# Queries of later tiles made in thirds and copied under masks, in a six-stage transformer kernel

## The reference

```python
q = (x @ Wq + bq).reshape(1, B * N, H, hd)            # H, hd = 16, 16
kv = (cond @ Wkv + bkv).reshape(1, -1, 2, H, hd)
...
q = _fq_sym(q, axis=-1)       # round(q/s), s = max|q|/127 over a head
k = _fq_sym(k, axis=-1)
v = _fq_sym(v, axis=2)
attn = jnp.einsum('bhqd,bhkd->bhqk', q, k)
attn = jax.nn.softmax(attn.astype(jnp.float32), axis=-1)
attn = _fq_unsigned(attn, axis=-1)
out = jnp.einsum('bhqk,bhkd->bhqd', attn, v)
return out @ Wp + bp
```

## Time and profile before

| | us |
|---|---|
| median of 3 runs | 464.66 |
| lowest and highest | 461.84, 470.23 |
| the profiled execution | 469.39 |
| its span, first to last instruction | 467.6 |
| TensorE busy in the span | 379.8 (81%) |
| VectorE busy | 302.8 (65%) |
| ScalarE busy | 213.5 (46%) |
| GpSimd busy | 133.1 (28%) |

### The profile page before, as it was taken

One profiled execution on the slowest core, in us unless ns is written; L12 is line 12 of the kernel. 1 busy time (PEld: TensorE's weight loads), 2 busy tenths in 40 slices (PEclk: granted clock), 3 DMA queues, 4 the chain that ended last, 5 costly groups with the idle time before them and its releaser, 6 DMA issues.

```text
span 467.6 us, 6836 instructions
## 1 busy us (share of the span) xinstructions
PE 379.8 (81%) x2363; PEld 225.6 (48%) x2387; DVE 302.8 (65%) x624; ACT 213.5 (46%) x546; POOL 133.1 (28%) x236
## 2 busy tenths in 40 slices
PE   5997878479977999989947558677666998999993
PEld 2646466334434566556624234324344644555562
DVE  4994398958734687878866989979861452122235
ACT  2655131272245765856435669898971311111100
POOL 8248756828671000020053441211110000000002
PEclk9979795779999799999976898988985698999997
DMA  8992101490000000000024656997996004012211
GB/s 249 329 359 22 1 2 1 147 393 1 0 1 0 1 2 1 1 2 1 2 53 63 131 104 114 175 167 145 153 164 203 0 0 147 22 45 64 50 45 45
DMA packets 75521, 39.84 MB, mean 85 GB/s; under 512 B 64160, under 2 KB 71264, under 8 KB 75040
## 3 DMA queue, kind: packets, MB, share of 16 engines
q1 hardware_dynamic: 73184, 39.35, 34.4%
q0 software_dynamic: 2304, 0.07, 1.5%
HBM read 21.58 MB, written 2.88 MB: 52 GB/s over the span
## 4 chain that ended last, share of the span: by engine, by line
PE 55%; DVE 19%; issue 9%; DMA 6%; ACT 5%; POOL 5%; SPq 0%; POOLq 0%; DVEq 0%; ACTq 0%
PE ps L819 28%; PE ps L1266 6%; PE ps L1002 5%; PE ps L1017 4%; DVE area_a L1642 4%; PE ps L1140 3%; DMA area_b<-area_b 3%; POOL deltas L506 2%; ACT area_b L744 2%; DVE area_b L1543 2%; PE ps L996 2%; PE ps L1036 2%; PE ps L1165 2%; DVE stats L1390 2%; DMA area_b<-deltas 1%
## 5 line engine op out<-in xcount | busy, mean ns | idle before, releaser
L744 ACT ACTIVATE area_b<-area_a,small 128x1024 int16<-128x1024 f32 x64 | 72.9, 1141 | 23.9 <-POOL small L578 20.1
L1642 DVE CUSTOM_DVE_ANT_0 area_a<-ps,zero,small 128x1024 f32<-128x1024 f32 x64 | 79.5, 1276 | 6.7 <-ACT area_b L744 4.5
L714 ACT ACTIVATE area_a<-ps,small 128x256 f32<-128x256 f32 (+1 forms) x128 | 51.9, 435 | 29.4 <-DVE small L1534 27.2
L475 POOL TENSOR_SCALAR var_eps<-meanvar 128x1 f32<-128x1 f32 x24 | 6.7, 280 | 199.8 <-DVE meanvar L1391 199.7
L819 PE MATMUL ps<-xT_odd,early 128*128 128x512 f32 x128 | 59.4, 612 | 0.0
L1714 DVE TENSOR_TENSOR area_b<-ps,area_b 128x512 f32<-128x512 f32 x16 | 11.1, 691 | 55.5 <-ACT area_b L794 55.5
L1140 PE MATMUL ps<-area_b 128*128 128x512 bf16 x86 | 29.0, 417 | 15.5 <-DVE small L1642 14.1
L1534 DVE TENSOR_REDUCE small<-ps 128x4 f32<-128x1024 f32 (+1 forms) x24 | 29.3, 1221 | 18.5 <-PE ps L1002 18.2
L794 ACT ACTIVATE area_b<-ps 128x512 f32<-128x512 f32 x16 | 9.5, 596 | 67.1 <-PE ps L819 67.1
L819 PE MATMUL ps<-area_b,xT_even 128*128 128x512 f32 x64 | 31.2, 632 | 9.0 <-ACT area_b L691 9.0
L819 PEld LDWEIGHTS ps<-xT_odd,early 128*128 128x128 f32 x128 | 24.9, 197 | 27.0 <-issue 26.5
(11 more groups left out here) (274 smaller groups left out, 685.3 us busy)
## 6 DMA issues: line engine op xcount, KB each, us to landing
early<-in_w_up_dram SPq DMA_DIRECT2D x1, 4096.0 KB, 16.0
area_b<-gates_out SPq DMA_DIRECT2D x16, 256.0 KB, 3.1
deltas<-area_b SPq DMA_DIRECT2D x1, 2112.0 KB, 17.6
area_b<-deltas SPq DMA_DIRECT2D x2, 1024.0 KB, 5.8
area_a<-in_w_down_dram SPq DMA_DIRECT2D x1, 2048.0 KB, 9.0
early<-in_ctxT_dram SPq DMA_DIRECT2D x1, 1024.0 KB, 13.7
early<-in_ctx_dram SPq DMA_DIRECT2D x1, 1024.0 KB, 13.9
early<-in_w_qkv_dram SPq DMA_DIRECT2D x2, 384.0 KB, 5.4
```

Source lines behind the costliest of these rows:

```text
L714: a = act.activation(p1[:, n % 2, x * nk * P:(x + 1) * nk * P], scores1(n)[:, x * nk * P:(x + 1) * nk * P], ACT.Exp, bias=nmx1[:, n % 2, x ...
L744: act.activation(px[:, u % PX, :], sx[u % 3], ACT.Exp, bias=nbx[:, u:u + 1], accum_out=zx[:, i, h:h + 1]).then_inc(sem("px_ready"), 1)
L1642: dve.tensor_tensor_reduce(sx[u % 3], bank(2 * (u % 2), 2), zero[:].broadcast_to([P, B * M]), qsc[:, i, h:h + 1], LOWEST, ALU.add, ALU.max ...
```

## The change

- Queries of tiles 1 to 3 are made eight units apart in place of five. `quantise_queries` is cut into `take_queries`, `scale_queries`, `round_queries` at steps 5, 6, 7; `stack_queries` into three at steps 8, 9, 10; turning and copying come at step 11, as does `add_bias`.
- All of their PSUM is in bank 4; `turn` of the units for ScalarE keeps bank 5 alone. `turn_x4` no longer waits for `res4_ready`; a wait for it stands before `apply` of the second tile.
- `take_even` and `take_odd` read all 128 partitions and multiply by a column of `half_sel` (1 in one half of the partitions, 0 in the other), so they write the zeros themselves. `take_odd` now waits for `take_even`. The memsets of `qTx` and `qT_first` go; `qstack` has two places, cleared once in stage 4.
- The last local tile: `turn_z1` comes behind `scores(0)`, `spread_z1` behind `scores(2)`, `take_z1` between maxima 0 and 1, `add1` one unit later, `norm_scale` three later.

The diff, cut to its core:

```diff
+        half_sel = sb("half_sel", [P, 2])
...
-        qstack = carve("a", 0, [TT, HX * KW], BF16)
+        qstack = carve("a", 0, [2, HX * KW], BF16)
...
         def later_tile(u, step):
-            i, at = divmod(u - step, 5)
+            i, at = divmod(u - step, 8)
         def by_scalar(u):
...
+            pool.memset(half_sel[:], 1.0)
...
+            link(select(half_sel[:, 0:1], [[0, 1]], KW - 1, -1, ALU.is_ge, 0.0))
+            link(select(half_sel[:, 1:2], [[0, 1]], -KW, 1, ALU.is_ge, 0.0))
...
-            def stack_queries(i):
-                pool.wait_ge(sem("q_rounded"), i + 1)
-                stack = qstack[:, i, :].rearrange("p (h w) -> p h w", w=KW)
+            def stack_queries(i, k):
+                if k == 0:
+                    pool.wait_ge(sem("q_rounded"), i + 1)
+                if k == 0 and i >= 2:
+                    pool.wait_ge(sem("qT_ps"), i - 1)
+                stack = qstack[:, i % 2, :].rearrange("p (h w) -> p h w", w=KW)
-                for k in range(3):
-                    q = pool.tensor_scalar(stack[:, :, k * DHX:(k + 1) * DHX], heads, -127.0, None, ALU.max)
-                q.then_inc(sem("qstack_ready"), 1)
+                pool.tensor_scalar(stack[:, :, k * DHX:(k + 1) * DHX], heads, -127.0, None, ALU.max).then_inc(sem("qstack_ready"), 1)
...
-                            stack_queries(0)
+                            for k in range(3):
+                                stack_queries(0, k)
-                    pool.wait_ge(sem("o1_ps"), len(items1) // 2)
-                    pool.memset(qstack.rearrange("p i (h w) -> p (i h) w", w=KW)[:, HX:, 3 * DHX:KW], 0.0)
                     for u in range(TT * HX):
-                        if u < 4:
-                            pool.memset(qTx[:, 2 * u:2 * u + 2], 0.0).then_inc(sem("qTx_cleared"), 1)
-                        if u == 4:
+                        if u == 6:
-                        if later_tile(u, 6):
-                            add_bias(later_tile(u, 6))
-                        if later_tile(u, 7):
-                            stack_queries(later_tile(u, 7))
+                        for k in range(3):
+                            if later_tile(u, 8 + k):
+                                stack_queries(later_tile(u, 8 + k), k)
+                        if later_tile(u, 11):
+                            add_bias(later_tile(u, 11))
...
-                    pool.memset(qT_first[:], 0.0).then_inc(sem("first_cleared"), 1)
-                    pool.memset(qstack[:, 0, :], 0.0)
+                    pool.memset(qstack, 0.0)
...
-                        act.wait_ge(sem("first_cleared"), 1)
             def take_x4(i):
-                act.activation(xT[0][:, :, i * P:(i + 1) * P], bank(7)[:, 0:D].rearrange("p (c t) -> p c t", c=DC),
+                act.activation(xT[0][:, :, i * P:(i + 1) * P], bank(7 if i == 0 else 4)[:, 0:D].rearrange("p (c t) -> p c t", c=DC),
             def take_even(i, b):
-                dst = qT_first[0:KW, :, 0, :] if i == 0 else qTx[0:KW, :, 0, i * P:(i + 1) * P]
-                act.activation(dst, bank(b)[0:KW].bitcast(BF16).rearrange("p (c t) -> p c t", c=HX // 2),
-                               ACT.Copy).then_inc(sem("qT_even"), 1)
+                dst = qT_first[:, :, 0, :] if i == 0 else qTx[:, :, 0, i * P:(i + 1) * P]
+                act.activation(dst, bank(b).bitcast(BF16).rearrange("p (c t) -> p c t", c=HX // 2),
+                               ACT.Copy, scale=half_sel[:, 0:1]).then_inc(sem("qT_even"), 1)
             def stage5():
                 for u in range(TT * HX):
...
-                    if later_tile(u, 8):
-                        act.wait_ge(sem("qTx_cleared"), 4)
-                        take_even(later_tile(u, 8), 7)
+                    if later_tile(u, 11):
+                        take_even(later_tile(u, 11), 4)
...
-                act.activation(pTx[u % PT], bank(4 + n % 2).bitcast(I16), ACT.Copy).then_inc(sem("pTx_act"), 1)
+                act.activation(pTx[u % PT], bank(5).bitcast(I16), ACT.Copy).then_inc(sem("pTx_act"), 1)
             def evac_sums(i):
...
             def turn_x4(i):
-                if i:
-                    pe.wait_ge(sem("res4_ready"), TT)
-                    mm = pe.transpose(bank(7)[:, c * P:(c + 1) * P], x_tok[0][:, i, c * P:(c + 1) * P], ident[:])
+                    mm = pe.transpose(bank(7 if i == 0 else 4)[:, c * P:(c + 1) * P], x_tok[0][:, i, c * P:(c + 1) * P], ident[:])
             def project_q(i):
-                dense(bank(7)[:, D:2 * D], tile_of(4, i), lambda d: wqx[:, d, :]).then_inc(sem("qx_ps"), 1)
+                dense(bank(7 if i == 0 else 4)[:, D:2 * D], tile_of(4, i), lambda d: wqx[:, d, :]).then_inc(sem("qx_ps"), 1)
             def turn_q(i, b):
-                pe.wait_ge(sem("qstack_ready"), i + 1)
+                pe.wait_ge(sem("qstack_ready"), 3 * (i + 1))
-                    mm = pe.transpose(bank(b).bitcast(BF16)[:, c * P:(c + 1) * P], qstack[:, i, c * P:(c + 1) * P], ident_b[:])
+                    mm = pe.transpose(bank(b).bitcast(BF16)[:, c * P:(c + 1) * P], qstack[:, i % 2, c * P:(c + 1) * P], ident_b[:])
             def stage5(turn_z1, spread_z1, project1):
...
-                    if n > 2:
-                        pe.wait_ge(sem("pTx_act"), n - 2)
+                    if n > 1:
+                        pe.wait_ge(sem("pTx_act"), n - 1)
-                        mm = pe.transpose(bank(4 + n % 2).bitcast(BF16)[:, k * P:(k + 1) * P],
+                        mm = pe.transpose(bank(5).bitcast(BF16)[:, k * P:(k + 1) * P],
...
-                for u in range(3):
-                    scores(u)
+                scores(0)
+                turn_z1(TT - 1)
+                scores(1)
+                scores(2)
+                spread_z1(TT - 1)
                 for u in range(units + 3):
-                    if u == 0:
-                        turn_z1(TT - 1)
-                    if u == 1:
-                        spread_z1(TT - 1)
-                    if later_tile(u, 8):
-                        turn_q(later_tile(u, 8), 7)
+                    if later_tile(u, 11):
+                        turn_q(later_tile(u, 11), 4)
...
-                        pe.wait_ge(sem("qT_even"), TT)
-                        pe.wait_ge(sem("qT_odd"), TT)
+                        pe.wait_ge(sem("res4_ready"), TT)
...
-                        dve.wait_ge(sem("first_cleared"), 1)
...
-            def quantise_queries(i):
-                scale = DHX ** -0.5
-                flat = qx[:, i, :]
-                heads = flat.rearrange("p (h d) -> p h d", d=DHX)
+            def take_queries(i):
-                TTN(out=flat, in0=bank(7)[:, D:2 * D], in1=bqx[:], op=ALU.add).then_inc(sem("qx_ready"), 1)
+                TTN(out=qx[:, i, :], in0=bank(7 if i == 0 else 4)[:, D:2 * D], in1=bqx[:], op=ALU.add).then_inc(sem("qx_ready"), 1)
-                link(dve.tensor_reduce(qam[:, i, :], heads, AX.X, ALU.max, apply_absolute_value=True))
-                link(TS(qsc[:, i, :], qam[:, i, :], scale / 127, 1e-8, ALU.mult, ALU.max))
+                link(dve.tensor_reduce(qam[:, i, :], qx[:, i, :].rearrange("p (h d) -> p h d", d=DHX), AX.X, ALU.max,
+                                       apply_absolute_value=True))
+            def scale_queries(i):
+                heads = qx[:, i, :].rearrange("p (h d) -> p h d", d=DHX)
+                link(TS(qsc[:, i, :], qam[:, i, :], DHX ** -0.5 / 127, 1e-8, ALU.mult, ALU.max))
-                link(TS(flat, flat, scale, ROUND, ALU.mult, ALU.add))
+            def round_queries(i):
+                flat = qx[:, i, :]
+                link(TS(flat, flat, DHX ** -0.5, ROUND, ALU.mult, ALU.add))
+            def quantise_queries(i):
+                take_queries(i)
+                scale_queries(i)
+                round_queries(i)
             def take_odd(i, b):
-                dve.wait_ge(sem("qT_ps"), i + 1)
-                dst = qT_first[KW:2 * KW, :, 1, :] if i == 0 else qTx[KW:2 * KW, :, 1, i * P:(i + 1) * P]
-                dve.tensor_copy(dst, bank(b)[KW:2 * KW].bitcast(BF16).rearrange("p (c t) -> p c t", c=HX // 2)).then_inc(sem("qT_odd"), 1)
+                dve.wait_ge(sem("qT_even"), i + 1)
+                dst = qT_first[:, :, 1, :] if i == 0 else qTx[:, :, 1, i * P:(i + 1) * P]
+                TS(dst, bank(b).bitcast(BF16).rearrange("p (c t) -> p c t", c=HX // 2), half_sel[:, 1:2], None,
+                   ALU.mult).then_inc(sem("qT_odd"), 1)
             def stage5(take_z1, normalise1, add1):
...
+                take_z1(TT - 1)
                 for u in range(units):
-                    if u == 0:
-                        take_z1(TT - 1)
-                    if u == 2:
+                    if u == 3:
-                    if u == 4:
+                    if u == 7:
-                        quantise_queries(later_tile(u, 5))
-                    if later_tile(u, 8):
-                        dve.wait_ge(sem("qTx_cleared"), 4)
-                        take_odd(later_tile(u, 8), 7)
```

(7 more changed lines are left out.)

## The result

| | before | after |
|---|---|---|
| median, us (20 runs each, taken together) | 466.12 | 462.81 |
| ratio, 95% interval | | 0.9905 [0.9876, 0.9934] |
| profiled execution, us | 469.39 | 462.97 |
| its span, us; mean granted clock | 467.6; 0.888 | 461.2; 0.91 |

By the ratio, which compares runs on the same chip, the change gains 4.4 us of 466.12 (3.1 to 5.8); the plain medians differ by 3.3. The gain is under 2%, but its interval excludes that nothing changed. The forecast was a gain of 3.5 and a median of 461.2, with a range of 455.5 to 467.5; the median is 462.81. The ratios rest on the faster executions of each kernel alone, and of the profiled ones those of before (469.39, which e11 repeats) and of e1 (465.37) lie just over 1.5% above the fastest execution of their kernel.

The account below looks back on a forecast made before the run. No engine bounds the kernel everywhere; VectorE is busiest in stage 5. Minus 6.2, plus 0.6 - 1.3 + 0.9, plus 2.2, plus 0.3 gave minus 3.5: from median 464.66 to 461.2 us, range 455.5 to 467.5.

Parts of the forecast that it names:

- The start: Last local tile's steps at stage 5's start: reordering removes VectorE's waits for TensorE, first query step at 11.8; minus 6.2 us.
- 0 by themselves, but they must be gone: GpSimd's dropped memsets between the first biases: no gain of their own, but the start's count needs them gone.
- Thirds: Queries of tiles 1 to 3 in three pieces: turn-arounds 0.6, ScalarE's hole minus 1.3, late bias 0.9; net plus 0.2 us.
- Serial copies: Stage 5, take_odd waits for take_even: VectorE stands 0.9 to 1.0 us three times, less 0.7 before; plus 2.2 us.
- Unit 27: Last tile's take_odd, right in front of add(0): covered but for a fraction by ScalarE's exponentials; plus 0.3 us.
- The lower end of minus 8: The most favourable extreme of the summed change in time, against plus 3 at the other end.
- From unit 30 on nothing is changed: Stage 5 behind maximum 30: same pace to maximum 63 and untouched tail; counted as 0.
- Maximum 0 against stage 4: A sign of being wrong: stage 5's first maximum moving by over 0.5 us relative to stage 4.
- (a): Rival: stage 5's gain is given back, as late exponentials delay maximum 12 and the copy, 3 x 1.2 us; 464.7; chance 0.20.
- (b): Rival: all VectorE's idle time from 236.7 to 283.4, 9.9 us, goes; 454.8; chance 0.10.
- (c): Rival: TensorE's queue jams at units 12 and 20 where turn_x4 waits for both copies; 471; chance 0.08.
- (d): Rival: the new start order doesn't take effect, TensorE's data as late as before, 4.7 of 6.2 missing; 466; chance 0.07.

Follow-up runs that it names:

- e11: The kernel before, unedited, run and profiled again as a control; ratio to the kernel before 0.9999.
- e1: The kernel before with only the new order of the last local tile's steps (and the unit at which GpSimd inverts its deviation); ratio to before 0.9941.
- e12: The changed kernel, unedited, run and profiled again as a control; ratio to the kernel before 0.9901, median 462.69 us.
- e7: The changed kernel with the four memsets of the query buffer put back among GpSimd's first biases, both copies waiting for them; ratio to before 0.9965.
- e5: The changed kernel with the two 64-partition copies side by side again and the cleared buffers they need; ratio to the kernel before 0.9928.
- e3: The changed kernel with queries back in one block five units apart, masked copies and bank 4 kept; ratio to the kernel before 0.9984.
- e6: The changed kernel with the masked odd copy of tiles 1 to 3 made twice over the same places; ratio to the kernel before 1.0005.
- e10: The changed kernel with tiles nine units apart, odd copy one unit later, add_bias at step 6, stacking at 9, 9, 10; ratio to before 0.9964.

## Why the prediction was right, and where it was off

- **The start, minus 6.2.** Right in mechanism and near in size: waits of 0.81, 2.28 and 1.63 gone, 1.70 down to 0.43, q1 at 11.86 against 11.8 forecast. The gain at q1 is 6.4 in the first pair of profiles and 5.4 in e11 and e12, of which 0.3 is the deferred `norm_scale`. The waits that the forecast names come to 4.7 + 1.2 = 5.9; for the other 0.3 of its 6.2 it names nothing. "0 by themselves, but they must be gone" held for the memsets: e7 prices them at 1.14 at the start.
- **Thirds, plus 0.2 (0.6 - 1.3 + 0.9).** The turn-arounds cost nothing: the three pieces of tile 1 hold VectorE for 0.92, 0.95 and 0.53 us (from each piece's start to the maximum behind it, without the deferred `norm_scale`), 2.40 in all, where the block took 2.41. Maximum 12 waited 0.24 in tile 1 and not at all in the others, where 0.3 each was taken. Both terms were sized too high. The waits for exponentials fell from 1.2 to 0.24, so this part came to about minus 1.0 in place of plus 0.2.
- **Serial copies, plus 2.2.** Waits of 3.4 in place of 0.7, plus 2.7. Between e7 and e5 it is 2.5. The masked copy took 0.751 against 0.7 assumed and 1.28 as the end, so the range's plus 1.8 is excluded.
- **Unit 27, plus 0.3.** The wait is 1.19 against 1.0 assumed; what the cover gives back lies behind maximum 30 (below).
- **Up to maximum 30** the gain was 5.2 in this pair of profiles and 4.4 in e11 and e12, against 3.5 forecast. What follows q1, the deferred `norm_scale` included, was forecast at plus 3.0 and came to 1.2 and 1.1: the thirds were cheaper, and 0.86 us that VectorE had waited before maxima 22, 24 and 28 of the kernel before is gone too. The lower end of minus 8 doesn't follow from the ends that the forecast gives for its parts; they add up to about minus 5.
- **"From unit 30 on nothing is changed"** failed as a step: it put this part at 0, and it gave 1.8 and 2.8 us. No instruction differs, but m30-m63 fell from 48.63 and 49.13 to 46.81 and 46.35. VectorE's waits in that stretch show where (after, then before; waits by line from maximum 30 to 63):

```profile
DVE area_a L1651 <- ACT area_b L747: 1.3, 3, 0.7
...
DVE area_a L1651 <- PE ps L1139: 1.0, 3, 0.5
```

```profile
DVE area_a L1642 <- ACT area_b L744: 2.8, 5, 1.0
...
DVE area_a L1642 <- PE ps L1140: 1.4, 3, 0.8
```

  In the kernels five units apart VectorE runs free from unit 20 or so and meets the slower ScalarE near unit 37, waiting there for exponentials (0.35, 0.20, 0.87 in before; 0.49, 0.20, 0.76 in e3; 0.44, 0.20, 1.14 in e1). With tile 3 made eight units apart, ScalarE catches up while VectorE stands at unit 27, and only the 0.20 is left. The eight profiles at eight units have 46.1 to 47.5, the four at five units 47.9 to 49.1 (nine units apart, tile 3's own steps fall into this stretch). The two groups don't overlap, and e3, which differs from the change in the spacing and packing alone, falls with the second; that points to the spacing, though at the nearest they are only 0.3 apart. The catching up is argued.
- **Maximum 0 against stage 4** was to move by no more than 0.5 us, and moved by 1.7 in some profiles. From the reduction of the table it is 75.3 us in four profiles before and with half copies, and in six with the masked copy, but 77.0 in after, e6, e10 and e12. Compare after (first two lines of TensorE, then VectorE) with e3:

```profile
210.61 1.03 PE L1117 MATMUL ps<-ident_b,area_a 128*128 128x128 bf16 x8 [1.50 <-DVE area_b L1540]
211.44 2.02 PE L821 MATMUL ps<-wo,area_b 128*128 128x256 f32 x4
```

```profile
212.82 0.75 DVE L1636 TENSOR_SCALAR qT_first<-ps,half_sel 128x1024 bf16<-128x1024 bf16 x1 [2.27 <-ACT qT_first L737]
...
215.34 1.22 DVE L1531 TENSOR_REDUCE small<-ps 128x4 f32<-128x1024 f32 x1 [1.76 <-PE ps L1004]
```

```profile
208.14 0.62 PE L1117 MATMUL ps<-ident_b,area_a 128*128 128x128 bf16 x8 [1.50 <-DVE area_b L1540]
208.60 1.08 PE L821 MATMUL ps<-wo,area_b 128*128 128x256 f32 x4
```

```profile
209.95 0.75 DVE L1636 TENSOR_SCALAR qT_first<-ps,half_sel 128x1024 bf16<-128x1024 bf16 x1 [1.86 <-ACT qT_first L737]
211.23 1.23 DVE L1531 TENSOR_REDUCE small<-ps 128x4 f32<-128x1024 f32 x1 [0.53 <-PE ps L1004]
```

  The masked copy itself costs nothing here, as forecast: in e3 the next step comes when it came before (75.35 for 75.33). But in four profiles TensorE's clock fell to its lower level behind a wait of 1.50 us, and projection and transposes took 1.3 us longer. Before has the same wait and kept its clock.

So two of the three signs by which the forecast wanted to be found wrong came true, the moved maximum 0 and the changed pace behind maximum 30; the third, a masked copy of 1.3 us, did not. The start, the mask and their sizes held. That the whole came out so near to the forecast is in part luck: less was lost behind q1 and some 2 us was gained behind maximum 30, and 2.7 us of the gain in stage 5 don't show in the median.

**What stays open.** A gain of 7.1 between maxima 0 and 63 became 4.4 in the median. Two things lie on the other side, and their size would fit (0.7 and 2.3 us on average): the 1.65 us of stage 4 in four profiles of ten with masked copies (none of four without), and the reduction of the table, which starts at 160.9 to 161.4 in the three kernels built without `half_sel` and at 161.3 to 164.7, mean 163.4, in the eleven with it. The granted clock from 150 to 165 us was 0.77 to 0.89 in the former and 0.54 to 0.89 in the latter, and the delay goes with it: from stage 4's first row reduction (147.2 to 149.0 us) to the one of the table it takes 12.6 to 12.9 us in the four profiles with a clock of 0.89, 13.9 to 14.2 in the three with 0.77 and 15.8 to 16.5 in the seven with 0.66 or 0.54. All seven have `half_sel`, but so have four of the other seven. Whether the new constants or the addresses they shift bring this on, or fourteen profiles happened to fall so, no run tells.

Of the rivals, (a) is out by the interval, as is (b), and (c)'s jam didn't occur: `turn_x4` waited 1.33 us for the copy, and the only wait of VectorE for TensorE that followed was the 0.43 for the projection. (d) is out by q1.

## What to carry to other kernels

Where engines run in step, put the producer's work one unit ahead of the consumer, and read the gain from the waits at that point; then look also at what the same edit takes out from under cover, as here the memsets. A hole on an engine with slack is worth only what reaches the bound engine (2.7 us on ScalarE, 0.2 on VectorE), while one more dependency on the bound engine costs nearly in full (0.6 to 1.0 us a tile). When the scatter of whole runs is near the effect, compare stretches between the same two instructions, and count what lies ahead of them and behind them as well.
